# Raw tiles of Wo in homes of their own, two score rows in other slots, a wait by half tiles

## The reference

```python
mod = (_silu(c) @ wmod).reshape(2, 6, 1, -1)           # sa, ca, ga, sb, cb, gb
ga, gb = their sign * max(abs, 0.25)
h = _layernorm(x) * (1 + ca) + sa
q, k = rotary(h @ wq), rotary(h @ wk); v = h @ wv      # 32 heads of 32
probs = softmax(causal(q @ k.T / sqrt(32)))
x = x + ga * ((probs @ v) @ wo)
h = _layernorm(x) * (1 + cb) + sb
base = h @ W_base.T + b_base
gate = softmax(h @ W_gate.T); thr = sigmoid(h @ W_thr + b_thr) * 0.125
w = relu(gate - thr) / sum                              # per token, 8 experts
moe = einsum('nd,erd->ner', h, A_w) * w @ B_w * 2       # rank 16
x = x + gb * (base + moe)
```

## Time and profile before

| | |
|---|---|
| time, median of 3 runs | 1673.23 us (1672.37 to 1678.04) |
| profiled execution, its own time | 1676.43 us |
| its span in the trace | 1674.6 us |
| busy: PE | 1592.1 us (95%) |
| busy: ACT | 1029.7 us (61%) |
| busy: DVE | 969.2 us (58%) |
| busy: POOL | 615.9 us (37%) |
| chain of waits that ended last | PE 70%, DVE 8%, POOL 6%, DMA 6%, issue 5%, ACT 3% |

### The profile page before, as it was taken

How to read it: one execution, slowest core, us unless ns; L and a number is a source line. 1 busy time by engine, 2 the same in 40 slices (tenths; PEclk the granted TensorE clock), 3 DMA queues, 4 the chain that set the end, 5 groups by cost and what they waited for, 6 DMA issues and landing times.

```text
span 1674.6 us, 29440 instructions
## 1 busy us (share of the span) xinstructions
PE 1592.1 (95%) x9530; PEld 1179.9 (70%) x9530; DVE 969.2 (58%) x2932; ACT 1029.7 (61%) x2662; POOL 615.9 (37%) x485
## 2 busy tenths in 40 slices
PE   4889999999999999999999999998989999999996
PEld 2556767667677767777777777764668888888885
DVE  5627577686766646666666657555654545454533
ACT  1338888889889879898898898887511111110100
POOL 3533253443533414324234234244214343434332
PEclk9999999999999999999999999995899999999998
DMA  9673444445443393243243333324621212111110
GB/s 345 224 251 85 111 104 108 121 114 143 114 106 91 75 284 77 60 103 85 67 100 75 81 80 83 77 74 129 169 89 38 75 50 63 53 62 57 56 63 25
DMA packets 172162, 174.43 MB, mean 104 GB/s; under 512 B 21172, under 2 KB 120804, under 8 KB 172024
## 3 DMA queue, kind: packets, MB, share of 16 engines
q1 hardware_dynamic: 169912, 168.55, 36.0%
q10 hardware_dynamic: 2112, 4.19, 0.8%
HBM read 96.65 MB, written 25.18 MB: 73 GB/s over the span
## 4 chain that ended last, share of the span: by engine, by line
PE 70%; DVE 8%; POOL 6%; DMA 6%; issue 5%; ACT 3%; SPq 1%; DVEq 0%; POOLq 0%; ACTq 0%
PE ps_s L1245 14%; PE ps_qkv L1245 13%; PE ps_s L1287 10%; PE ps_pv L1314 9%; PE ps_t L1256 8%; PE ps_s L690 5%; PE ps_qkv L662 3%; PE ps_s L662 3%; DMA x<-in_L_attn_x_dram 2%; POOL h_lo L897 1%; DMA x_start<-in_L_attn_x_dram 1%; DVE rows_sb L1762 1%; DMA out_dram<-x 1%; POOL x L912 1%; POOL xn L910 1%
## 5 line engine op out<-in xcount | busy, mean ns | idle before, releaser
L1502 ACT ACTIVATE rows_sb<-rows_sb,bias_m 128x640 f32<-128x640 f32 (+7 forms) x512 | 396.1, 774 | 12.5
L1762 DVE CUSTOM_DVE_ANT_0 rows_sb<-ps_t,mask 128x512 f32<-128x512 f32 (+3 forms) x512 | 296.8, 586 | 166.4 <-PE ps_t L1256 160.5
L1538 ACT ACTIVATE probsT<-ps_s 128x512 f32<-128x512 f32 (+2 forms) x640 | 321.2, 542 | 40.7 <-PE ps_s L1287 24.2
L1256 PE MATMUL ps_t<-stk 96*128 96x512 f32 (+3 forms) x768 | 271.1, 356 | 10.7 <-DVE smax L1762 7.6
L1287 PE MATMUL ps_s<-stk 98*128 98x512 f32 (+3 forms) x768 | 231.1, 382 | 4.0 <-ACT probsT L1538 3.6
L1788 DVE TENSOR_TENSOR ps_s<-ps_s,mask_t 128x128 f32<-128x128 f32 (+1 forms) x384 | 120.7, 340 | 173.1 <-PE ps_s L1287 168.9
L1287 PEld LDWEIGHTS ps_s<-stk 98*128 98x128 f32 x768 | 130.4, 193 | 89.3 <-issue 52.5
L1256 PEld LDWEIGHTS ps_t<-stk 96*128 96x128 f32 x768 | 148.0, 193 | 62.1 <-DVE smax L1762 14.6
L1916 POOL TENSOR_TENSOR rope_b<-rope_b,rope_sin 128x512 f32<-128x512 f32 x64 | 82.8, 1294 | 281.7 <-DVE rope_b L1747 281.7
L1314 PE MATMUL ps_pv<-probsT,v_all 128*32 128x256 f32 (+1 forms) x2816 | 185.2, 358 | 0.0
L1245 PE MATMUL ps_qkv<-hT_hi,w_hi 128*128 128x512 f32 x384 | 158.3, 412 | 7.9 <-DVE hT_lo L1722 3.7
(11 more groups left out here) (211 smaller groups left out, 3048.3 us busy)
## 6 DMA issues: line engine op xcount, KB each, us to landing
stk<-rot SPq DMA_DIRECT2D x384, 128.0 KB, 2.4
probsT<-in_L_wmod_dram SPq DMA_DIRECT2D x5, 2048.0 KB, 11.7
wm_one<-in_L_wmod_dram SPq DMA_DIRECT2D x5, 2048.0 KB, 14.6
w_raw<-in_L_attn_wq_dram SPq DMA_DIRECT2D x16, 512.0 KB, 4.1
w_raw<-in_L_attn_wk_dram SPq DMA_DIRECT2D x16, 512.0 KB, 4.7
w_raw<-in_L_attn_wv_dram SPq DMA_DIRECT2D x16, 512.0 KB, 4.3
attn_scratch<-attn_sb SPq DMA_DIRECT2D x128, 64.0 KB, 3.2
h_scratch<-h_pair SPq DMA_DIRECT2D x32, 256.0 KB, 3.0
```

The source lines that it names most:

```text
L1256: pe.matmul(bank[:, 0:c1 - c0], stk[0:3 * HD, u % 2, 0, qt // 4, h, qt % 4 * P:(qt % 4 + 1) * P], stk[0:3 * HD, u % 2, 1, part, h, 0:c1 - ...
L1502: act.activation(row, row, ACT.Exp, bias=bias_m[:, qt, h:h + 1], scale=SCALE, accum_out=sums[:, qt // 4, h, qt % 4:qt % 4 + 1]).then_inc(s ...
L1538: act.activation(probsT[:, w % 4, hs[0]:hs[-1] + 1, 0:n], s_bank[(NS * u + k) % 3][:, 0:len(hs) * n].rearrange("p (h n) -> p h n", h=len(hs)),
L1762: dve.tensor_tensor_reduce(rows_sb[:, to, at + c0:at + c1], bank[:, 0:n], mask[:, BANK - n:BANK] if last else mask[:, 0:1].broadcast_to([P ...
```

## The change

It has seven parts.

1. `ROW_SLOTS`: slot 4 issues three rows and not two, slots 7 and 8 two rather than three, slot 9 three. Rows 10, 12 and 14 thus stand a slot earlier and row 19 a slot later; by `EXPS` the exponential of the whole row that row 19 ends moves by a slot too.
2. Wo's eight raw tiles get eight homes, laid over `x_next`, `h_pair` and buffers of raw and split weights of the projections that are done with by then. All eight are loaded in half period 28, and POOL's split waits only for its own tile.
3. `project(0)` moves to half period 30, three products behind each of the rows 8 to 23; `project(1)` takes its place in slots 3 to 11 of half period 31.
4. The residual is cut into `gate` and `residual`. For tile 0, DVE makes gate, residual and norm in slots 2, 4 and 6 of half period 31, and PE transposes xn in slot 10.
5. Behind the last values PE has only the last 14 pieces to transpose; ACT and DVE make a half of h2 and a part of the pieces in turns.
6. SP: `load_early` and `load_ga` stand earlier in half period 30, x for the first two tiles ahead of `place_m` in half period 31, three pieces earlier, the last six pieces ahead of the waits for the last stores, and B comes in 4 transfers a half, not 8. POOL waits for the store of a chunk of attention output ahead of tile 0's split.
7. In the body PE waits for each half of h2 ahead of its four blocks, not for both at once.

```diff
-ROW_SLOTS = {0: 2, 1: 2, 2: 2, 3: 2, 4: 2, 5: 2, 6: 2, 7: 3, 8: 3, 9: 2, 10: 2}
+ROW_SLOTS = {0: 2, 1: 2, 2: 2, 3: 2, 4: 3, 5: 2, 6: 2, 7: 2, 8: 2, 9: 3, 10: 2}
...
-        wo_raw = [x_next[:, :], h_pair[:, :, :].rearrange("p a n -> p (a n)")]
...
+        staging = ExitStack()
+        staging.enter_context(nc.sbuf_tensor("wo_skip", [P, 3, KT, S], F32))
+        wo_st = [staging.enter_context(nc.sbuf_tensor("wo_st0", [P, 2, D], F32)),
+                 staging.enter_context(nc.sbuf_tensor("wo_st1", [P, 2, D], F32))]
+        staging.enter_context(nc.sbuf_tensor("wo_skip_v", [P, KT, P], F32))
+        wo_st.append(staging.enter_context(nc.sbuf_tensor("wo_st2", [P, 2, D], F32)))
+        wo_raw = [x_next[:, :], h_pair[:, :, :].rearrange("p a n -> p (a n)")]
+        wo_raw += [w[:, a, :] for w in wo_st for a in range(2)]
+        staging.close()
...
-        wo_ld = [sem(f"wo_ld{i}") for i in range(3)]
+        wo_ld = [sem(f"wo_ld{k}") for k in range(KT)]
...
-        n_dma = {("bt", 0): E_, ("ag", 1): 1 + AGW - ER - E_}
+        n_dma = {("bt", 0): KT // 2, ("ag", 1): 1 + AGW - ER - E_}
...
-                for e in range(E_):
-                    sp.dma_start(v[:, :, e, :], B_w[e].rearrange("(t p) r -> p t r", p=P)[
-                        :, 4 * half:4 * half + 4, :]).then_inc(ld, 16)
+                for j in range(KT // 2):
+                    at = (4 * half + j) * P
+                    sp.dma_start(v[:, j, :, :], B_w[:, at:at + P, :].rearrange("e p r -> p e r")).then_inc(ld, 16)
...
-            sp.wait_ge(wo_lo_ok, KT)
+            sp.wait_ge(wo_lo_ok, 2)
...
+            for n in range(2 * len(stage), UNITS):
+                load_piece(sp, n)
...
-            for n in range(2 * len(stage), UNITS):
-                load_piece(sp, n)
...
-                pe.wait_ge(h2_hi_ok, 2 * i + 2)
-                pe.wait_ge(h2_lo_ok, 2 * i + 2)
...
+                        if c == 0 and kt % 4 == 0:
+                            pe.wait_ge(h2_hi_ok, 2 * i + kt // 4 + 1)
+                            pe.wait_ge(h2_lo_ok, 2 * i + kt // 4 + 1)
...
-            turn_weights(pe, 0)
-            project(pe, 1)
-            pe.wait_ge(st_lo, SOON)
-            turn_xn(pe, 0)
-            turn_weights(pe, 1)
+            for part in range(2):
+                turn_weights(pe, part)
...
-            split_weights(0)
-            split_h(0)
-            split_weights(1)
+            for half in range(2):
+                split_h_half(0, half)
+                split_weights(half)
             tile_loops(act, body)
-        def residual(dve, j, hp, e, b):
-
+        def gate(dve, j, b):
...
+        def residual(dve, j, hp, e):
...
-                    residual(dve, i + 1, *after(hp, e), bj)
+                    gate(dve, i + 1, bj)
+                    residual(dve, i + 1, *after(hp, e))
...
-            dve.wait_ge(rows_ld, 16 * B)
-            residual(dve, 0, 0, 0, 0)
-            rest_weights(dve, 0)
-            norm(dve, 0, 0)
-            modulate(0, 0)
-            rest_weights(dve, 1)
+            for half in range(2):
+                modulate_half(0, 0, half)
+                rest_weights(dve, half)
...
+            chunk_stored(pool, 2 * PAIRS - 2)
...
-                if k >= 2:
-                    sp.wait_ge(wo_lo_ok, k - 1)
-                sp.dma_start(wo_raw[k % 2], wo[k * P:(k + 1) * P, :]).then_inc(wo_ld[k % 2], 16)
+                sp.dma_start(wo_raw[k], wo[k * P:(k + 1) * P, :]).then_inc(wo_ld[k], 16)
...
+                if u == PAIRS - 1:
+                    sp.wait_ge(sum_ok, NW * PAIRS)
+                    for e in range(2):
+                        load_x1(sp, e, e)
...
+                if u == PAIRS - 4:
+                    sp.wait_ge(ln_tr, 4 * NT)
+                    for k in range(2):
+                        load_wo(k)
                 if u == PAIRS - 2:
-                    load_wo(5)
-                    load_wo(6)
+                    load_early(sp)
+                    load_ga(sp)
                 if u == PAIRS - 1:
-                    sp.wait_ge(sum_ok, NW * PAIRS)
-                    for e in range(2):
-                        load_x1(sp, e, e)
+                    for n in range(len(stage), len(stage) + 3):
+                        load_piece(sp, n)
...
-                    load_wo(2)
-                    load_wo(3)
-                if u == PAIRS - 2:
-                    load_wo(7)
+                if u == PAIRS - 4:
+                    sp.wait_ge(v_hi_ok, 2 * T)
+                    sp.wait_ge(v_lo_ok, 2 * T)
+                    for k in range(2, 4):
+                        load_wo(k)
...
-                    sp.wait_ge(ln_tr, 4 * NT)
-                    for k in range(2):
+                    sp.wait_ge(proj_mm, 6 * (T - 1) + 4)
+                    for k in range(4, KT):
                         load_wo(k)
-                if u == PAIRS - 3:
-                    load_wo(4)
-                if u == PAIRS - 2:
-                    load_early(sp)
...
-                    for n in range(len(stage), 2 * len(stage)):
+                    for n in range(len(stage) + 3, 2 * len(stage)):
...
-                    load_ga(sp)
...
+                        if u == PAIRS - 2 and k >= EARLY_ROWS:
+                            if k == EARLY_ROWS:
+                                pe.wait_ge(vT_ok, 2 * T)
+                                pe.wait_ge(wo_hi_ok, KT)
+                                pe.wait_ge(wo_lo_ok, KT)
+                            project(pe, 0, 3 * (k - EARLY_ROWS), 3 * (k - EARLY_ROWS + 1))
...
-                        if i == 3:
-                            pe.wait_ge(vT_ok, 2 * T)
-                            pe.wait_ge(wo_hi_ok, KT)
-                            pe.wait_ge(wo_lo_ok, KT)
-                        project(pe, 0, 6 * KT * (i - 3) // 9, 6 * KT * (i - 2) // 9)
+                        project(pe, 1, 6 * KT * (i - 3) // 9, 6 * KT * (i - 2) // 9)
...
+                    if u == PAIRS - 1 and i == SOON + 2:
+                        pe.wait_ge(st_lo, SOON)
+                        turn_xn(pe, 0)
...
+                    if u == PAIRS - 1 and i == 2:
+                        dve.wait_ge(rows_ld, 16 * B)
+                        gate(dve, 0, 0)
+                    if u == PAIRS - 1 and i == 4:
+                        residual(dve, 0, 0, 0)
+                    if u == PAIRS - 1 and i == 6:
+                        norm(dve, 0, 0)
...
-                    pool.wait_ge(wo_ld[k % 2], 16 * (k // 2 + 1))
-                    pool.tensor_copy(wo_hi[:, k, :], wo_raw[k % 2]).then_inc(wo_hi_ok, 1)
+                    pool.wait_ge(wo_ld[k], 16)
+                    pool.tensor_copy(wo_hi[:, k, :], wo_raw[k]).then_inc(wo_hi_ok, 1)
                     pool.wait_ge(wo_hi_ok, k + 1)
-                    pool.tensor_tensor(wo_lo[:, k, :], wo_raw[k % 2], wo_hi[:, k, :].bitcast(F32),
+                    pool.tensor_tensor(wo_lo[:, k, :], wo_raw[k], wo_hi[:, k, :].bitcast(F32),
```

## The result

The changed kernel took 1659.36 us (median of 4 runs, 1658.30 to 1662.46), the kernel before 1675.35 (median of 4, 1672.37 to 1678.04): a ratio of 0.9906, with a 95% interval of 0.9889 to 0.9923. That is 16.0 us faster, where 24.5 were forecast, and 1659.36 is 1.4 us above the forecast's range.

What follows compares the result with a forecast made beforehand. PE was taken to bound ordinary half periods (ACT 89% busy). Terms 8.0 + 1.1 + 0.5 − 1.2 + 15.2 + 0.9 = 24.5 us off the profiled 1676.43 gave 1651.9; the median, 3.2 lower, gave 1648.7 us, range 1642 to 1658.

Steps and rivals of the forecast that it cites:

- Part 1: Half periods 2 to 9: moving rows out of slots 7 and 8 removes PE's stall in slot 8, 8.0 us gained.
- what may be late next: Slot 9: row 21 needs row 19 read; margin some 0.3 us ordinarily, about nothing in the normalizing half periods.
- rival 1: Normalizing half periods: slot 8's stall only moves to slot 9, row 21 waiting for row 19; 1656.7 us, chance 0.13.
- Rival 3: Row 21 waits in slot 9 of all 31 half periods, 44.3 us of loss; 1701 us, chance 0.05.
- Part 2: Wo's homes and project(0) one half period earlier: slots 4 to 11 of half period 30 gain 1.1 us.
- 0.5 for m_col: DVE's m_col meets POOL's train at another phase in half period 30: 0.5 us of gain.
- rival 4: Half period 30: project(0) starts late because POOL or a Wo transfer is late, 5 us of PE wait; 1654, chance 0.08.
- the products cost nothing: Slots 4 to 11 of half period 30: 21.9 us with the 48 products at full clock, against 23.0 without.
- Part 3: Half period 31: project(1) replaces project(0), with a 0.3 us gate wait and 0.9 us of xn transposes; 1.2 us lost.
- Part 4: From last attention values to tile 0's first product: h2 made sooner, PE at the tile at 1224.5, 15.2 us gained.
- Part 5: Last output tile: first W_base products wait only for h2's first half, 0.9 us gained.
- My signs: Right: five trace marks, such as no smax wait in slot 8. Wrong: slot 9 third-row wait or POOL's split interrupted, over 1658.

Runs made afterwards that it cites:

- short_mod: Changed kernel with one DVE scaling in place of four in slot 7 of half periods 2 to 9, part of the modulation wrong: 1652.09 us.
- keep_busy: Changed kernel with 80 transposes of the identity into a free bank added on PE in half periods 29 and 30: 1655.45 us.
- after_again: The changed kernel once more, unedited: 1657.45 us.
- best_busy: Changed kernel with batch 1's scaling straight from the transposes' bank, gate(0) in slot 0 of half period 31, and 80 filler transposes on PE: 1641.87 us.

## Why the prediction was wrong

**Part 1, the row slots (8.0 us forecast, 0.1 to 0.5 measured in its half periods).** I priced the stall of the earlier trace rows as if it stood alone. The step that failed is "what may be late next": I asked whether row 21 would have to wait for row 19, found a margin, and kept the gain. Two trains start from the scaling of the earlier trace rows, and the order of the rows doesn't shorten them: DVE's, from the scaling to row 23, 9.3 us without a pause, and ACT's, from the cast behind the scaling, 11.9 us, from which slot 11's scaling, m_col and the next slot 0 follow. So PE's wait only went to slots 4, 9 and 0. My argument against rival 1 (rope and triangle are shorter than the scaling) compared two pieces of DVE's train, and ACT's I didn't look at. short_mod shows that a shorter scaling is worth 0.9 us a half period. Rival 1 was right that the gain doesn't come, but not on the wait: in slot 9 PE waits 0.74 us for ACT's exponential, not for row 19. Its time, 1656.7, is 2.7 below the result. Rival 3 did not come: in ordinary half periods slots 4, 8 and 9 changed by +0.24, −0.17 and +0.19 us, the length of a row.

**Part 2, project(0) in half period 30 (1.1 us of gain forecast, 4.4 of loss measured, and 5.7 of gain just ahead of it, where I had 0.5 for m_col).** POOL's train was priced well: its last subtraction ended at 1155.31, forecast 1155.9, and PE waited 0.71 us for it, so rival 4 did not come. The failing step is "the products cost nothing". I set 21.9 us at full clock against 23.0 us in the old trace, and that comparison had two faults. PE came to slot 4 at 1.2 GHz, so the first products took 0.43 us apart and not 0.23; and the 23.0 us without products were not what slots 4 to 11 need, since with the new row slots and no products u 30 takes 29.9 us, not 32.3. The products were charged to waits that another part of the same change removes. The 21.9 us weren't far off: with the clock held at 1.00 (keep_busy) slots 4 to 11 took 23.26, of which 1.08 are a wait for POOL. The gain of 5.7 us in u 29 comes from the slots and the homes too, and the sum had only m_col's 0.5 there.

**m_col.** The price of a POOL subtraction beside it held. In half period 30 it took 0.89 us (1.24 in after_again), where it had taken 2.10. But the same meeting now comes in half period 31, where I had written "before and after" alike: the split of the second attention tile waits for project(0) (POOL's a_hi began at 1178.41, behind PE's last product), which now ends there. DVE, POOL and PE of the changed kernel:

```profile
1180.40 1.51 DVE L1788 SCALAR_TENSOR_TENSOR m_col<-logs,smax 128x8 f32<-128x8 f32 x1
```

```profile
1179.53 2.36 POOL L898 TENSOR_TENSOR a_lo<-a_raw,a_hi 128x1024 fp32r<-128x1024 f32 x1
```

```profile
1182.06 0.36 PE L1272 MATMUL ps_t<-ident,m_col 128*8 128x128 f32 x1 [1.93 <-DVE m_col L1788]
```

Both end at 1181.9, and PE waits 1.93 us, not 1.39.

**Part 3 (1.2 us of loss forecast, 2.4 measured, at a mean clock of 0.94 before and after).** The transposes of xn took 1.04 us (0.9 forecast). The wait for the gate was mis-sized: 1.32 us, not 0.3. I had counted gate(0) from the end of project(0), and not the piece of W_base that stands ahead of it on DVE.

**Part 4 (15.2 us forecast, 14.98 measured).** This mechanism and its size were right: ACT came to the ten pieces at 1216.48 (forecast 1216.2), and from there to the tile were 8.81 us (8.35). Tile 0's first product came 13.59 us behind the values:

```profile
1225.29 0.47 PE L702 MATMUL ps_s<-wb_hi,h_hi 128*128 128x512 f32 x1 [2.02 <-DVE wb_lo L657]
```

It ends the same wait for the same DVE line as before. **Part 5** was right too: 0.86 us against 0.9, and the last tile waits for DVE and not for h2.

```profile
1633.95 0.77 PE L702 MATMUL ps_s<-wb_hi,h_hi 128*128 128x512 f32 x1 [4.22 <-DVE xn L868]
```

Tile 0 itself, 32.52 us against 30.89, is no cost of the change that I can show: the second execution took 30.22.

In sum: of the forecast's 24.5 us, parts 4 and 5 gave 15.8, part 1 nothing where it was expected, the stretches of parts 2 and 3 took 6.8, and the row slots and homes together gave back 5.7 in a place where the sum had 0.5.

My signs didn't catch it. All that were to show it right came: no wait for smax in slot 8, POOL's a_lo before 1157, the clock at 1.00 from 0.4 us into slot 5 of half period 30 on, tile 0 15.0 us sooner, a wait of 4.2 us ahead of the last tile. Neither sign of being wrong came, and the time was over 1658 all the same. That it is over by only 1.4 us is in part luck, since the 5.7 us in half period 29 make up for most of part 1.

## What to carry to other kernels

A wait on PE is worth its length only if what ends it can be done sooner: measure the unbroken train of work of the releaser, and of each engine that waits for the same thing, and compare them with PE's, before pricing a move of what waits. Work that is put into idle time has to be priced at the clock that PE has there, and against the idle time that is left once the other edits of the same change are in. Where PE pauses often, a few instructions without a use can be cheaper than the lower clock; here that is shown for one stretch (u 30a, 17.84 us against 19.37 to 20.63), not for the whole kernel's time.

## What the hardware showed that I had not expected

PE's granted clock was 0.50 over u 29b with the old slots, where PE was busy 16.5 of 18.2 to 19.8 us, and 0.74 to 1.00 with the new ones, where the same work took it 9.7 to 12.0 of 14.3 us. 80 transposes without a use held it at 1.00 up to the end of half period 30, in both kernels that have them. One kernel's executions differ by 2 to 14 us, and the slowest has in most cases the lowest mean granted clock, or shares it (best_busy: 0.992 at 1639.15 us, 0.983 at 1652.82).

An m_col of 8 columns on DVE took 0.15 us alone and 0.89, 1.51 and 2.10 us beside a POOL subtraction, and ended with it within 0.02 us each time.
